# The second level's mixture of experts: every expert on every token, or tokens sorted by expert into 38 tiles

## The reference, cut to what matters

```python
y = _cat_linear(x, itok_B_0_63, W, b)     # y[b] = x[b] @ W[cat[b]] + b[cat[b]], one 128x128 matrix per sequence
s_raw = y @ Wg                            # (4096, 8)
routed = softmax(s_raw[:, :7]);  shared = softmax(s_raw[:, 7:])
_, idx = top_k(routed, 1)                 # K - KS = 1: ONE routed expert per token, its gate renormalised to 1
for e in range(8):                        # experts 0..6 routed, 7 shared (gate 1)
    a, bgate = split(y @ Wl1[e], 2)       # 128 -> 512
    out += gate[:, e] * ((silu(bgate) * a) @ Wl2[e])    # 256 -> 128
x = x + out
```

## Time and profile before

| | us |
|---|---|
| runs | 6193.25, 6198.14, 6207.54 (median 6198.14) |
| profiled execution | 6195.72 |
| its span | 6193.9 |
| first load of `level1` issued, its last addition to x begun | 1255.87, 1736.29 |
| first product of `level2_cond` | 1739.34 |

### The profile page before, as it was taken

The page is one execution under the profiler, slowest core; times in us unless marked ns, Lnnn a source line. Parts: engine busy times, 40 slices in busy tenths (PEclk is TensorE's granted clock), DMA queues, the critical chain, the costliest instruction groups (busy, mean ns, idle before and its releaser), DMA issues. The chain is left out here.

```text
span 6193.9 us, 130018 instructions
## 1 busy us (share of the span) xinstructions
PE 5476.1 (88%) x43710; PEld 3342.3 (54%) x43710; DVE 3978.4 (64%) x6881; ACT 3394.8 (55%) x9864; POOL 3116.7 (50%) x1445
## 2 busy tenths in 40 slices
PE   5995997579979998999899989999999999987853
PEld 2332775334446664666466646664666466644531
DVE  2111002723358885888588858885888588856888
ACT  0000000411128994989499949994999488944432
POOL 0000000200038883888388848883888388840026
PEclk9999999578879999999999999999999999997975
DMA  7666553000000000000000000000000000000000
GB/s 213 184 156 152 109 106 75 1 28 5 14 20 1 0 0 19 1 0 0 19 1 0 0 19 1 0 0 19 1 0 0 19 1 0 0 16 12 7 3 11
DMA packets 254013, 188.00 MB, mean 30 GB/s; under 512 B 176798, under 2 KB 237342, under 8 KB 247398
## 3 DMA queue, kind: packets, MB, share of 16 engines
q1 hardware_dynamic: 191785, 118.57, 8.0%
q10 hardware_dynamic: 61885, 64.76, 3.7%
HBM read 127.19 MB, written 56.08 MB: 30 GB/s over the span
## 5 line engine op out<-in xcount | busy, mean ns | idle before, releaser
L1636 POOL TENSOR_TENSOR rs<-ss,minus_half 128x16 f32<-128x16 f32 x386 | 1127.8, 2922 | 282.2 <-DVE ss L1713 281.5
L1554 ACT ACTIVATE s_ps<-s_ps,low 128x128 f32<-128x128 f32 x3072 | 1051.3, 344 | 81.5 <-DVE low L1724 76.1
L1634 POOL TENSOR_TENSOR t<-t 128x1024 f32<-128x1024 f32 x386 | 910.1, 2358 | 160.5 <-DVE t L1702 159.8
L1641 POOL TENSOR_TENSOR qk<-t,rs 128x1024 f32<-128x1024 f32 x386 | 734.6, 1903 | 60.5 <-POOL rs L1636 23.7
L1554 ACT ACTIVATION_READ_ACCUMULATOR s_ps<-s_ps,low 128x1 f32 x3072 | 641.3, 209 | 0.0
L1724 DVE TENSOR_REDUCE low<-s_ps 128x4 f32<-128x512 f32 x768 | 494.5, 686 | 204.0 <-PE s_ps L1382 204.0
L1696 DVE TENSOR_TENSOR t<-qk_ps,rot 128x1024 f32<-128x1024 f32 x386 | 472.4, 1224 | 166.5 <-PE qk_ps L1348 151.7
L1733 DVE TENSOR_TENSOR p<-s_ps,rec 128x512 f32<-128x512 f32 x768 | 530.7, 691 | 30.5
L258 PE MATMUL h_ps<-h_x,h_w 9*128 9x512 bf16 x4096 | 439.6, 628 | 70.2 <-DMA h_w<-rows_w1s 61.1
L1388 PEld LDWEIGHTS pT_ps<-ident,p 128*128 128x128 f32 x3072 | 353.9, 141 | 266.9 <-issue 264.6
L1568 ACT ACTIVATE pT<-pT_ps 128x512 f32<-128x512 f32 x768 | 459.7, 599 | 59.8 <-PE pT_ps L1388 26.6
(11 more groups left out here) (359 smaller groups left out, 9170.1 us busy)
## 6 DMA issues: line engine op xcount, KB each, us to landing
h_x<-rows_xs SPq DMA_DIRECT2D x512, 72.0 KB
rows_hs<-h_parts ACTq DMA_DIRECT2D x88, 384.0 KB, 6.4
z_fm<-rows_hs SPq DMA_DIRECT2D x128, 144.0 KB
x_fm<-rows_hs SPq DMA_DIRECT2D x128, 144.0 KB
wqkv<-in_wqkv SPq DMA_DIRECT2D x7, 1536.0 KB, 6.8
o_w<-rows_exs ACTq DMA_DIRECT2D x512, 18.0 KB
rows_xs<-z_fm ACTq DMA_DIRECT2D x12, 384.0 KB, 5.2
rows_exs<-s_exp ACTq DMA_DIRECT2D x9, 512.0 KB, 12.2
```

The costliest lines, as they stand in the source:

```text
L1554: ins = act.activation(s_ps[:, e, i * P:(i + 1) * P], s_ps[:, e, i * P:(i + 1) * P], ACT.Exp, bias=low[:, c % 2, e, i:i + 1], scale=-1.0, ...
L1634: pool.tensor_tensor(t1[:, i, :], t1[:, i, :], t2[:, i, :], ALU.add).then_inc(s_["t12"], 1)
L1636: pool.tensor_tensor(rs[:, i, :], ss[:, i, :], R.minus_half[:, 0:2 * UH], ALU.pow).then_inc(s_["rs"], 1)
L1641: pool.tensor_tensor(qk[:, i, :].rearrange("p (h d) -> p h d", d=DH), t1[:, i, :].rearrange("p (h d) -> p h d", d=DH), rs[:, i, :].unsquee ...
```

## The change

The routed experts no longer run on all tokens. `level1` becomes a sequence of stages, written out without loops:

1. `condition` and `logits` for all 8 groups, PE and ACT taking turns. The bias now comes as ACT's bias operand. PE also turns y into token-major rows (L979), which ACT keeps (L1067). Expert weights, the fourth level's weights and the clearing of a 2.5 MB buffer in device memory are issued from ACT's queue.
2. A sort on DVE: two products on PE count the tokens of each expert up to each token (L985), and 30 small operations (L1184 to L1213) give every token its slot, and each of 38 tiles of 128 slots its expert. Every expert starts on a new tile; 38 tiles hold the worst case.
3. The shared expert on all tokens (PE L993, L1000), while POOL scatters the rows of y to their slots in device memory: 32 indirect transfers of 128 rows of 512 B.
4. The 38 tiles. SP fetches a tile, PE turns it, ACT copies it, PE multiplies it by the weights of the tile's expert, whose number is read into a register, then silu, product, two turns, a copy, two products, a copy, and SP stores the tile.
5. When all tiles are stored, POOL gathers the rows back, 32 indirect transfers again, and PE turns them, group by group, for DVE to add them to x.

```diff
+SLOTS = (TOK + (MOE - 1) * (SLOT - 1)) // SLOT          # 38
             def _(pool):
+                pool.wait_ge(cleared, dma_at(0))
+                pool.wait_ge(s_["ytc"], at(NG - 1))
+                pool.wait_ge(s_["slot"], at(0))
+                for b in range(B):
+                    pool.indirect_dma_start(T["sorted"], bass.IndirectOffsetOnAxis(sloti[:, b:b + 1], 0),
+                                            yt[:, b, :], None).then_inc(sorted_, 16)
+                pool.wait_ge(sorted_, 16 * B)
+                for c in range(4):
+                    pool.wait_ge(stored[c], dma_at((SLOTS - c + 3) // 4 - 1))
+                for b in range(B):
+                    pool.indirect_dma_start(yt[:, b, :], None, T["routed"],
+                                            bass.IndirectOffsetOnAxis(sloti[:, b:b + 1], 0)).then_inc(back[b // GB], 16)
             def _(sp):
+                sp.wait_ge(sorted_, 16 * B)
+                def fetch(i):
+                    sp.wait_ge(s_["ysT"], at(i - 4))
+                    sp.dma_start(rows[:, i % 4, :], T["sorted"][i * SLOT:(i + 1) * SLOT, :]).then_inc(loaded[i % 4], 16)
+                def store(i):
+                    sp.wait_ge(s_["orow"], at(i))
+                    sp.dma_start(T["routed"][i * SLOT:(i + 1) * SLOT, :], orow[:, i % 4, :]).then_inc(stored[i % 4], 16)
+                slots([(fetch, 0), (store, 4)], 4, SLOTS)
             def _(pe):
+                def turn(i):
+                    pe.wait_ge(loaded[i % 4], dma_at(i // 4))
+                    pe.wait_ge(s_["ysc"], at(i - 2))
+                    pe.transpose(turn_ps[i % 2][:, 0:SLOT], rows[:, i % 4, :], R.ident[:, :]).then_inc(s_["ysT"], 1)
+                def up_routed(i):
+                    experts[i] = pe.value_load(owner[0:1, i:i + 1], min_val=0, max_val=R_E - 1)
+                    pe.wait_ge(s_["ysc"], at(i))
+                    pe.wait_ge(s_["hr"], at(i - 2))
+                    pe.matmul(up_ps[i % 2][:, :], ys[:, i % 2, :],
+                              w1[:, bass.ds(experts[i], 1), :].rearrange("p a o -> p (a o)"), ...).then_inc(s_["zr"], 1)
+                def turn_hidden(i): ...      # waits hr(i), hTc(i - 2); two transposes
+                def down_routed(i): ...      # waits hTc(i), orow(i - 2); two products of 128 columns
+                slots([(up_routed, 1), (turn_hidden, 2), (down_routed, 3), (turn, 0)], 3, SLOTS)
+                def turn_back(j):
+                    pe.wait_ge(back[j], 16 * GB)
+                    ...
             def _(act):
+                slots([(silu, 1), (keep_hidden, 2), (keep_sorted, 0)], 2, SLOTS)
             def _(dve):
+                for k in range(NG):
+                    if k == 1: fp4_weights(0)
+                    if k == 5: fp4_weights(1)
+                    route(k)
...
+                slots([(shared, 0), (add_shared, 1), (quantise, 0)], 1, NG)
+                slots([(gated, 1), (keep_rows, 3)], 3, SLOTS)
```

More of the change, by code:

```diff
@@ L963, in _ @@
-                pe.wait_ge(weights, dma_at(1))
-                pipeline(pe, NG, 2, [(experts, 1), (condition, 0)])
+                        mm = pe.transpose(t_ps[:, seq(b)], y[:, seq(k * GB + b)], R.ident[:, :])
+                    mm.then_inc(s_["turned"], 1)
+                slots([(logits, 1), (condition, 0)], 1, NG)
+                pe.wait_ge(s_["gate"], at(NG - 1))
+                every = gate[:, :, :].rearrange("p b e -> p (b e)")
+                pe.matmul(g_ps[:, 0:ROUTED], tri[:, :], every, start=True, stop=True)
@@ new lines, in _, with up @@
+                pe.matmul(g_ps[:, ROUTED:2 * ROUTED], R.ones[:, :], every, start=True, stop=True
+                          ).then_inc(s_["count"], 1)
+                pe.wait_ge(weights, dma_at(1))
+                def up(k):
+                    for t in (2, 0, 3, 1):
+                        pe.wait_ge(s_["h"], at(k * 2 + t % 2 - 2))
+                        pe.matmul(z_ps[t][:, :], w1[:, R_E, t * P:(t + 1) * P], y[:, k * GT:(k + 1) * GT],
+                                  start=True, stop=True).then_inc(s_["z"], 1)
@@ L1084, in _, with o @@
-                pipeline(dve, NG, 2, [(experts, 1), (route, 0)])
+                    dve.wait_ge(s_["gate"], at(k))
+                for k in range(NG):
+                    if k == 1:
+                        fp4_weights(0)
+                    if k == 5:
+                        fp4_weights(1)
+                    route(k)
+                sorts = 0
+                def o(ins):
+                    nonlocal sorts
+                    ins.then_inc(s_["sort"], 1)
+                    dve.wait_ge(s_["sort"], at(sorts))
+                    sorts += 1
@@ new lines, in _ @@
+                dve.wait_ge(s_["count"], at(0))
+                within, total = (g_ps[:, n * ROUTED:(n + 1) * ROUTED].rearrange("p (b e) -> p b e", b=B) for n in range(2))
+                o(dve.tensor_copy(run[0][:, :, :], total.rearrange("p b e -> p e b")))
+                a, c = run
+                for d in (1, 2, 4, 8, 16):
+                    dve.tensor_copy(c[:, :, 0:d], a[:, :, 0:d])
+                    o(dve.tensor_tensor(c[:, :, d:B], a[:, :, d:B], a[:, :, 0:B - d], ALU.add))
+                    a, c = c, a
```

407 lines of the change are left out of this document (242 added, 165 removed).

## The result

The changed kernel takes 5981.94 us (median of 4 runs, 5973.02 to 5988.07) against 6202.84 (4 runs on the same chip, 6193.25 to 6210.44): ratio 0.9644, 95% interval 0.9623 to 0.9664. That is 221 us less by these medians, 208 by the two profiled executions (5988.07 against 6195.72). The forecast was 172 less, 6026, from 5975 to 6135: the direction and the range held. The forecast time was 44 us too long; the saving came out 49 us above the forecast, since the kernel before took 5 us more here than in the runs that the forecast had.

What follows compares the result with a forecast made beforehand. PE's work was taken as the bound (437 of 482 us busy); five rebuilt stages ended the phase at 1565 instead of 1737, 172 us less: 6024 against the profiled 6195.7, median 6026, range 5975 to 6135.

Steps and rivals of the forecast that it cites:

- 5 gather, last turn, hand-over to the next stage: End of level1: gather 32 × 1.5 + 2 = 50 us, last turn and addition 2, clearing semaphores 1.5; ends at 1565.
- the price of a tile: Stage 4: 2.5 us at 2.4 GHz, 4.4 at 1.2, taken as 3.2; 38 tiles plus 6 for filling and draining, 128 us.
- Rival A: Cheap descriptors and fast clock: transfer 0.8 us, tiles 2.5, stage 1 at 5.7 per group; 5966 us, chance 0.14.
- The price of a group: Stage 1, conditioning: a chain without overlap, 5.7 us fast, 7.4 slow, taken as 6.5; eight groups 52 us.
- Stage 3: Shared expert 41 us plus some 4, beside the scatter's 50 us, which is 5 us longer; ends at 1378.
- The transfer's price: POOL's indirect transfers in scatter and gather: 1.5 us each, between bounds 0.35 and 2.9, as a software loop over 128 rows.
- The rule weighed in the prediction: Stage 3: DVE's fast two-port copies or TENSOR_SCALARs lock GpSimd out of writing descriptors; up to 5 us longer, gather no longer.
- Outside it nothing changes: Everything outside the phase from 1256 to 1737 us was taken to keep its time.
- a part outside `level1` that moves by more than 2 us: One of the listed signs that the prediction would be wrong.
- B: Tiles run at 1.2 GHz: 4.4 instead of 3.2 us, +46, and stage 1 at 7.4 per group, +7; 6079 us, chance 0.14.
- C: Scatter and gather: transfer 2.9 us, +90, 6116 us; or each lands before the next, +115, 6141 us; chance 0.17.
- D: Indirect transfers not spread over 16 engines: 5.3 us per 128 rows, scatter 172 instead of 50, gather too; 6270 us, chance 0.08.

Runs made afterwards that it cites:

- adapter loads moved: SP's 64 adapter loads moved from beside the scatter into the tile loop, two per tile, against the changed kernel: 5985.4 us, ratio 0.9652.
- late scatter: POOL starts the scatter only when the shared expert is done, against the changed kernel: 6020.34 us, ratio 0.9714.
- early turn: PE turns the next tile right behind the first layer and ACT copies it out first, against the changed kernel: 5959.24 us, ratio 0.9617.
- late clearing: Clearing of the sorted rows moved behind the third conditioning group on ACT's queue, against the changed kernel: 5993.25 us, one run.
- six buffers: Early turn plus six row buffers instead of four, stores two tiles later, against the changed kernel: 5956.6 us on chip 15; 5982.17 us, ratio 0.9632, on chip 10.
- all together: Early turn, six buffers, late clearing, and quantising moved behind the tiles, against the changed kernel: 5959.37 us, ratio 0.9591.

## Why the prediction was right in direction and short in size

By its own stages, in the profiled execution of the changed kernel (forecast, measured, from the level's first load on):

| stage | forecast | measured | what it was |
|---|---|---|---|
| 1 conditioning | 62 | 56.7 | start 15.1 instead of 9; a group 5.76 at 1.2 GHz, 3.7 at 2.4, instead of 6.5 |
| 2 sort | 10 | 8.7 | |
| 3 shared expert, scatter, first fetch | 52 | 65.4 | 17 us of late hand-overs; without them 44.7 to 48.7; counted from the start of the operation that writes the slots |
| 4 tiles, last store | 131 | 93.4 | 2.35 us a tile instead of 3.2; some 2 us for filling and draining instead of 6 |
| 5 gather, last turn, hand-over to the next stage | 56 | 49.7 | 1.25 us a transfer instead of 1.5; from the last addition's end to the next stage 4.9 instead of 3.9 |

The 44 us are the level's 37 and the 12 by which the stage behind it was shorter, less 14 because this execution reached the level later; the remaining 9 are where the two profiled executions lie among their runs (the forecast added 2.4 to the profiled time for the median; the median lies 6.1 below it).

**The step that failed is the price of a tile**, 38 × (3.2 − 2.35) = 32 of the level's 37 us. The working from the rows gave 2.5 us at 2.4 GHz, right to 6%; the 0.15 that it was over are 6 of the 32. The other 26 are the clock, which raised it to 3.2. I put the tiles between two stretches of the earlier trace rows, 52% busy at 0.57 and 81% busy at 0.93. The tile stage is 80% busy and was granted 1.00. Lower values stood only at its start in the six executions in which PE had stood idle for 2 us or more ahead of the first tile (0.73 to 0.86 over the first 25 us: adapter loads moved, late scatter, early turn, late clearing, the first with six buffers, all together), and 0.93 over the last 25 us with the adapter loads moved. The row at 81% and 0.93 was the nearest one by busy share, its 2.7 us a tile would have given 19 us of the 44, and I left it for a middle between two far ends. Busy share alone does not settle it either way: conditioning, 74% busy, was granted 0.50 up to 1316 us. Rival A, whose tiles run at the full clock for 2.5 us, came nearest (5966), in part by luck: its price of a transfer, 0.8 us, was further off than the forecast's.

**The price of a group held by errors that offset each other.** The logits' 1.88 us stood in the sum for 2.4 GHz and in that for 1.2 GHz alike. They were measured at 1.2 (kernel before; the clock is the 0.50 behind the busy times), and take 1.06 at 2.4 (changed kernel, last group):

```profile
1682.00:1685.00 3.00, 1.88 (x8) 1.78 (x8) 0.63 (x4) 0.30 (x1) 0.00 (x0) 0.50 0.00 0
```

```profile
1323.95 1.06 PE L974 MATMUL g_ps<-moe_wg,y_cat 128*128 128x8 f32 x8 [1.23 <-ACT y_cat L1061]
```

The four products without their bias products take 1.91 us at 1.2 GHz and 1.06 at 2.4, where 2.9 and 1.7 were priced. So a group is 5.76 us at 1.2 GHz, priced 7.4, and 3.7 at 2.4, priced 5.7. Six of the eight began at 1.2 GHz, and the stage's first product came 6 us later than priced: the sum was 5 us off.

**Stage 3 was near for what it considered, and late hand-overs came on top.** In four profiles without late hand-overs (early turn, late clearing, early turn with six buffers, all together) it took 48.4, 48.3, 48.7 and 44.7 us from the slots to the first tile. In five others, of code that is the same up to there but for the row buffers, it took 63.2 to 68.8. The difference, 17 us, does not belong to the program as built: the kernel with six buffers had both. Whether it belongs to the single execution or to the chip, no run parts. The five are the changed kernel's first profile and all four profiles with a full scatter from chip 10; the seven without late hand-overs are all from chips 5 and 15, the six-buffer kernel's first among them. For the execution speaks only that one of that kernel's five runs on chip 10 took 5954.36 us and the others 5980.83 to 5991.98.

That scatter and adapter loads must meet has lost its ground. The three kernels in which they did not meet ran on chip 5, where the early turn, in which they do, had no late hand-over either. And in the same five executions, in no other, the last one or two hand-overs from PE to DVE in the gather are late too, by 0.6 to 4.2 us where 0.04 to 0.11 is usual, with no adapter load near. The last addition to x in the changed kernel, where PE's turn had ended at 1536.09, and in the first profile with six buffers, where it had ended at 1506.65:

```profile
1537.72 0.69 DVE L1248 TENSOR_TENSOR x_fm<-x_fm,ytok_ps 128x512 f32<-128x512 f32 x1 [4.92 <-remote]
```

```profile
1506.69 0.69 DVE L1248 TENSOR_TENSOR x_fm<-x_fm,ytok_ps 128x512 f32<-128x512 f32 x1 [4.31 <-PE ytok_ps L1041]
```

What is shown of the scatter's late hand-overs is that they begin 4 to 10 us behind the start of the scatter's first transfer and end 3 to 5 us behind the start of its last one in all five, that PE, ACT, DVE and SP are all late, and that POOL and the DMA engines (19% busy) are not. The cause stays open.

**The transfer's price** was taken as 1.5 and is 1.25 in the gather and 1.27 in a scatter alone, 1.34 to 1.40 beside DVE's quantising. The reason given, a loop over 128 rows, was wrong: the gather of 64 rows shows a price that hardly depends on them. The rule weighed in the prediction (the Trainium skill, SBUF — State Buffer, "Who interferes with whom") gave up to 5 us, by the prediction's estimate, for DVE's copies and TENSOR_SCALARs beside the scatter. The runs show 4 us, and for the TENSOR_SCALAR over 1536 elements that a transfer ends right behind it. The transfer begun at 1475.92 had only TENSOR_TENSORs beside it and took 1.95 us too. The Trainium skill says in the same section that a TENSOR_TENSOR with both inputs in SBUF contends with GpSimd's reads, and infers that the writing of descriptors is not held up by it; here the transfers beside such operations were longer all the same (three of 1.49 to 2.02 us in the first profile with six buffers). Which part of a transfer waits, no run shows.

**"Outside it nothing changes"** cost 12 us: `level2_cond` took 51.6 us for 63.9. Both profiles of the kernel before have 63.9; of the new ones seven have 51.6 to 52.3 and five 64.1 to 68.7, and the kernel with six buffers had each. So the code of the phase alone does not decide it, though how often it comes out short may: the two at 68.7 are the two kernels with the late clearing. Chip 10 gave both 52.0 and 64.1, so the chip alone does not decide it either. With it goes the granted clock: 0.86 over the stage at 51.6 to 52.3 us, 0.69 at 63.9 to 64.2, 0.62 at 68.7. The prediction named a part outside `level1` that moves by more than 2 us as a sign of being wrong; for this program it should have held that stage as ±12 us, and the place of the level's first load too (1255.9 and 1259.3 before, 1258.3 to 1272.0 after).

**Of the rivals**, B (tiles at 1.2 GHz), C (2.9 us or landing one after another) and D (transfers on few engines) are out: 1.00 granted, transfers 1.25 us apart that land after 2.5, so that the landing counts once.

## What to carry to other kernels

Where dense masked work is replaced by sorted tiles, price a tile once at each of the two clocks and keep the two sums apart, with a chance for each, instead of pricing a middle between far rows; and see that each row is used for the clock that it was measured at. Then look at the order inside the tile: turning the next tile right behind the first product and letting the fetches lead by the number of buffers took it from 2.35 to 1.85 us, more than the register read (0.08) or the clearing (nothing). That is the stage's gain; in the kernel's time on one chip it did not come clear of the noise. A queue that issues loads in order sets the pace as soon as its round is longer than the tile, so what is moved off a disturbed stretch must not go there. And when one profile shows a disturbance, repeat the same program, on the same chip and on another, before explaining it: two of them here, 17 and 12 us, changed between two profiles of one program, and since these were from two chips, they do not say which of the two did it.

## What the runs showed of the hardware that was not expected

- An indirect transfer by GpSimd of 128 rows of 512 bytes costs 0.945 us busy and 0.30 between (0.905 for 64 rows), and lands after 2.5 us in the gather, 2.2 in a scatter alone.
- Beside DVE's operations over 1536 elements, TENSOR_TENSOR among them, single transfers took 1.11 to 2.79 us busy in the ten profiles with both; the first transfer of a scatter took 1.31 in any case.
- PE's read of an index into a register costs 0.08 us a tile where PE waits for a copy anyway.
- While a scatter ran beside the shared expert, the other engines' hand-overs came late in five of nine executions, with one wait of 17.7 us where 2.8 is usual. The four of the five whose chip is known were on chip 10; none of the four without was.
- The same stage of one program, from its first product on, got 2.4 GHz after 9 us in one execution and after 34 in another, with PE as little busy in the 38 us ahead (7.4 and 7.6 us, granted 0.50).
